# Keys made with tokens on partitions in a two-layer efficient-attention kernel

## The reference

```
xn = layernorm(x)
q, k, v = xn @ Wq + bq, xn @ Wk + bk, xn @ Wv + bv       # 512 x 512 each
k = k where the token is valid, else -inf (layer 0) or k - 1e6 (layer 1);  v = v * valid
q = softmax over the features of a head;   k = softmax over the tokens
att = k^T v for each head                                  # 16 heads of 32, then 8 of 64
y = q att;  h = layernorm(y) * (1 + scale(cond)) + shift(cond)
x = x + silu(h) @ Wout + bout
```

## Time and profile before

| what | value |
|---|---|
| median of 3 runs | 861.52 us (857.33 to 862.12) |
| the profiled execution | 857.14 us |
| its span in the trace | 855.1 us |
| PE busy | 838.2 us (98%) |
| DVE, ACT, POOL busy | 679.3, 603.1, 548.9 us |
| granted TensorE clock | full, in every slice |
| moved by DMA | 169.81 MB, 199 GB/s on average |

### The profile page before, as it was taken

The page is one execution under the profiler, slowest core; times in us unless marked ns, Lnnn a source line. Parts: engine busy times, 40 slices in busy tenths (PEclk is TensorE's granted clock), DMA queues, the critical chain, the costliest instruction groups (busy, mean ns, idle before and its releaser), DMA issues.

```text
span 855.1 us, 20095 instructions
## 1 busy us (share of the span) xinstructions
PE 838.2 (98%) x6659; PEld 719.9 (84%) x6659; DVE 679.3 (79%) x1362; ACT 603.1 (71%) x1442; POOL 548.9 (64%) x741
## 2 busy tenths in 40 slices
PE   7999999999999999999999999999999999999998
PEld 7778888888888888888878888888888888888886
DVE  6987778778788788778887887787788787787766
ACT  5376687686676776686876886776776686676665
POOL 3467766766766666766767667667667666765641
PEclk9999999999999999999999999999999999999999
DMA  8876676766667756555587556656566656566441
GB/s 309 286 225 201 201 218 199 228 216 205 195 210 208 233 197 199 179 165 175 169 247 233 185 172 200 201 180 201 179 204 201 202 186 189 178 194 211 142 160 62
DMA packets 139404, 169.81 MB, mean 199 GB/s; under 512 B 12302, under 2 KB 112006, under 8 KB 139302
## 3 DMA queue, kind: packets, MB, share of 16 engines
q1 hardware_dynamic: 138512, 167.56, 62.5%
q10 hardware_dynamic: 790, 0.98, 0.4%
HBM read 95.61 MB, written 72.88 MB: 197 GB/s over the span
## 4 chain that ended last, share of the span: by engine, by line
PE 83%; DMA 6%; DVE 4%; issue 2%; SPq 2%; POOL 1%; ACT 1%; DVEq 0%; POOLq 0%; ACTq 0%
PE PS L1152 72%; PE PS L1248 6%; PE PS L1232 3%; DMA X<-in_x 2%; DMA XT<-x_turned 1%; DMA x_turned<-XS 1%; DMA k_turned<-KT 1%; DMA QT<-qy_turned 1%; POOL XL L667 0%; SPq L400 0%; PE PS L1322 0%; DMA EK<-k_turned 0%; DVE BNX L1515 0%; PE PS L1276 0%; PE PS L1291 0%
## 5 line engine op out<-in xcount | busy, mean ns | idle before, releaser
L680 POOL TENSOR_TENSOR HL<-H,HH 128x512 fp32r<-128x512 f32 x60 | 77.5, 1292 | 185.3 <-ACT HH L916 185.3
L867 ACT ACTIVATE Z<-QT,FC,FA 128x128 f32<-128x128 f32 x240 | 99.0, 483 | 87.7 <-DMA QT<-qy_turned 87.7
L1152 PE MATMUL PS<-XH,WH_k 128*128 128x256 f32 x512 | 149.8, 293 | 0.7 <-DVE KN L1581 0.7
L1152 PE MATMUL PS<-XL,WH_k 128*128 128x256 f32 x512 | 144.8, 283 | 0.0
L1152 PE MATMUL PS<-XH,WL_k 128*128 128x256 f32 x512 | 144.8, 283 | 0.0
L953 ACT ACTIVATE XN<-X,NBX,RSX 128x512 f32<-128x512 f32 x60 | 48.8, 813 | 85.5 <-POOL NBX L629 85.5
L829 ACT ACTIVATE SK<-SK,KN 128x128 f32<-128x128 f32 x256 | 98.9, 387 | 10.7 <-DVE KN L1581 10.4
L1152 PE MATMUL PS<-WH_o,HH 128*128 128x512 f32 x248 | 101.3, 408 | 2.0 <-issue 1.9
L1152 PE MATMUL PS<-WH_v,XH 128*128 128x512 f32 x256 | 100.8, 394 | 0.0
L1152 PE MATMUL PS<-WH_q,XH 128*128 128x512 f32 x256 | 100.7, 393 | 0.0
L1152 PE MATMUL PS<-WL_v,XH 128*128 128x512 f32 x256 | 100.3, 392 | 0.0
(11 more groups left out here) (171 smaller groups left out, 2106.6 us busy)
## 6 DMA issues: line engine op xcount, KB each, us to landing
qy_turned<-QS SPq DMA_DIRECT2D x60, 512.0 KB, 2.9
QT<-qy_turned SPq DMA_DIRECT2D x240, 128.0 KB, 3.1
EK<-k_turned SPq DMA_DIRECT2D x128, 128.0 KB, 2.8
x_turned<-XS SPq DMA_DIRECT2D x30, 512.0 KB, 3.3
XT<-x_turned SPq DMA_DIRECT2D x120, 128.0 KB, 3.5
k_turned<-KT SPq DMA_DIRECT2D x52, 256.0 KB, 3.8
out_x<-X SPq DMA_DIRECT2D x31, 256.0 KB, 3.2
X<-in_x SPq DMA_DIRECT2D x11, 512.0 KB, 5.3
```

The costliest lines, as they stand in the source:

```text
L680: eng.tensor_tensor(hl_of(o), h_of(o), hh_of(o).bitcast(F32), ALU.subtract).then_inc(pool_hl, 1)
L867: z = eng.activation(z_of(o)[:, c * P:c * P + P].rearrange("p (q n) -> p q n", q=Q), src, ACT.Identity, bias=FC[l][:, c, b:b + 1], scale=F ...
L1152: mm = eng.matmul(dst, left[a](c), right[b](c), start=(c == 0 and a + b == 0), stop=(c == C - 1 and a == 1))
```

## The change

`keys(i)` now computes one tile's keys with tokens on partitions and features in the columns, through `project_x`, as values and queries do: 12 matmuls of 512 columns. ACT copies the bank to SK and adds the tile's mask, which is now one number for each token (`keep_keys`). The maxima over tokens go across partitions: DVE turns SK in 32 x 32 blocks (KT) and reduces each to 16 numbers (`key_maxima`, PM), PE transposes PM of a pair of tiles (`turn_max`), DVE reduces over the four groups of tokens and rounds as the key bias would (`row_maxima`, NM, 32 x 32), SP writes NM to memory and reads it back onto all 128 partitions (`write_max`, `spread_max`, MX, 128 x 1024). POOL subtracts MX (`shift_keys`), ACT takes one exponential of 512 columns (`exp_k`), and SK is used in attention where it lies.

Sums are no longer taken before attention. Each head's values have a column of ones beside them (VV is 33 or 65 columns a head), so attention's last column is the sum; DVE divides after attention (`scale_heads`, into HT), and POOL spreads HT over the head's place in ATT by multiplying it with a 0/1 pattern DG (`heads`), two instructions of 256 columns. The zeroing of PSUM, the masks in MB, EK and its transfers are gone. The lists are rewritten in even and odd steps; attention of all tiles from 4 to 61 is done in pairs.

```diff
             def keys(i):
 
-                g, p = divmod(i, 2)
-                l = i // B
+                g, t = divmod(i, 2)
...
-                    eng.wait_ge(dve_ka, i - 1 if i in (2, B + 2) else i)
-                xs = [lambda c: XH[g % 2][:, c, :], lambda c: XL[g % 2][:, c, :]]
-                for cc in range(2):
-                    f = (2 * p + cc) * P
-                    ws = [lambda c: WH[0][:, c, f:f + P], lambda c: WL[0][:, c, f:f + P]]
-                    dst = bank(bank_k(i), cc * PAIR, PAIR)
-                    mm = split_product(dst, ws, xs, fresh=(4 * l if i % B == 0 and cc == 0 else None))
-                mm.then_inc(pe_k, 1)
+                    eng.wait_ge(act_ka, i - 1 if i == 2 else i)
+                project_x(i, 0, bank(bank_k(i)), pe_k)
...
+            def turn_max(g):
+                eng.wait_ge(dve_pm, 2 * g + 2)
+                if g == 0:
+                    eng.wait_ge(act_xf, 3)
+                else:
+                    eng.wait_ge(dve_hd, max(2 * g - 1, 2))
+                eng.transpose(PS[0:D // 16, B_ATT, 0:P], PM[:, :, :].rearrange("p t n -> p (t n)"), ident[:, :])\
+                   .then_inc(pe_pm, 1)
...
+            def even_step(s):
+                keys(s)
+                values(s)
+                for j in attention_at(s):
+                    attention(j)
+                keys(s + 1)
+                queries(s)
+                output(s - 4)
+                turn_max(s // 2)
+                mix(s - 2)
+            def odd_step(s):
+                values(s)
...
+                queries(s)
...
+                output(s - 4)
+                mix(s - 2)
...
+            def key_maxima(i):
...
+                then(eng.transpose(KT[:, :].rearrange("p (a n) -> p a n", n=32),
+                                   SK[:, i % 3, :].rearrange("p (a n) -> p a n", n=32)))
+                eng.wait_ge(pe_pm, g)
+                eng.tensor_reduce(PM[:, t, :], KT[:, :].rearrange("p (a n) -> p a n", n=32), AX.X, ALU.max)\
+                   .then_inc(dve_pm, 1)
...
+            def row_maxima(g):
...
+                then(eng.tensor_reduce(NM[:, :], PS[0:D // 16, B_ATT, 0:P].rearrange("p (q n) -> p n q", q=Q), AX.X, ALU.max))
+                then(eng.tensor_tensor(NM[:, :], NM[:, :], bk, ALU.add))
+                eng.tensor_tensor(NM[:, :], NM[:, :], bk, ALU.subtract).then_inc(dve_km, 1)
...
+            def shift_keys(i):
+                eng.wait_ge(ld_mx, 16 * (i // 2 + 1))
+                sk = SK[:, i % 3, :]
+                eng.tensor_tensor(sk, sk, MX[:, i % 2, :], ALU.subtract).then_inc(pool_kn, 1)
...
+            def write_max(g):
+                eng.wait_ge(dve_km, g + 1)
+                eng.dma_start(KD, NM[:, :]).then_inc(st_km, 16)
+            def spread_max(g):
+                eng.wait_ge(st_km, 16 * (g + 1))
+                eng.wait_ge(pool_kn, 2 * g)
+                src = KD.rearrange("(o a) n -> o (a n)", o=1)
+                eng.dma_start(MX[:, :, :].rearrange("p t n -> p (t n)"), src.partition_broadcast(P)).then_inc(ld_mx, 16)
```

More of the change, by code:

```diff
@@ L742, in _ @@
-            for s in range(5, B - 1):
-                step(s)
-            add_bo(31)
-            root_y(28)
-            root_x(36)
-            split_low(eng, 4, [1])
-            x_low(33)
-            normalise_keys(31)
-            mask_of_keys(16)
-            queries(31)
-            h_low(27)
+            def odd_step(s):
+                h_low(s - 4)
+                root_y(s - 3)
+                if s > 5:
+                    heads(s - 2)
+                x_low(s + 2)
+                for n in stats_at(s):
+                    root_x(n)
+                shift_keys(s - 1)
+                shift_keys(s)
+                queries(s)
+                if s == 5:
+                    heads(s - 2)
@@ L753, in _ @@
+            odd_step(5)
+            for s in range(6, B - 2, 2):
+                even_step(s)
+                odd_step(s + 1)
+            even_step(30)
+            x_low(33)
+            split_low(eng, 4, [1])
+            h_low(27)
+            root_y(28)
+            heads(29)
+            queries(31)
+            shift_keys(30)
+            shift_keys(31)
+            root_y(29)
+            heads(30)
+            root_x(37)
             h_low(28)
-            root_y(29)
-            normalise_keys(32)
@@ L788, in _ @@
+            add_bo(33)
+            even_step(34)
+            odd_step(35)
             split_low(eng, 7, [1])
-            root_x(41)
             split_low(eng, 7, [3])
-            normalise_keys(36)
-            queries(36)
-            x_low(38)
-            for s in range(B + 5, NT - 2):
-                step(s)
+            for s in range(B + 4, NT - 2, 2):
+                even_step(s)
+                odd_step(s + 1)
             add_bo(62)
             root_y(59)
+            heads(60)
@@ L1024, in step, with odd_step @@
                     norm_x(n)
+                exp_k(s - 2)
+                exp_k(s - 1)
+                keep_keys(s)
+                norm_y(s - 3)
                 film(s - 4)
+                exp_q(s - 2)
+                values(s)
+                h_high(s - 4)
+                keep_keys(s + 1)
+                x_turned(s + 2)
+                film(s - 3)
+            def odd_step(s):
+                if s == 5:
+                    film(1)
+                h_high(s - 4)
+                exp_q(s - 2)
+                for n in norm_at(s):
+                    norm_x(n)
+                x_turned(s + 2)
@@ L1026, in step @@
                 norm_y(s - 3)
-                x_turned(s + 2)
-                h_high(s - 4)
                 if s in FILM_SLOTS:
                     conditioning_sums(FILM_SLOTS.index(s))
-                exp_k(s)
-                exp_q(s - 2)
-                heads(s - 2)
                 values(s)
-            for s in range(5, B - 1):
-                step(s)
-            norm_x(35)
+            odd_step(5)
+            for s in range(6, B - 2, 2):
+                even_step(s)
+                odd_step(s + 1)
@@ L1123, in _ @@
             values(t2)
+            exp_k(62)
             exp_q(t1)
-            heads(t1)
+            exp_k(63)
             norm_y(t0)
@@ L1391, in _ @@
             count()
+            turn_max(0)
             keys(2)
@@ L1408, in _, with even_step, odd_step @@
             keep_busy(B_K, 2)
-            def step(s):
-                keys(s)
+            keys(4)
+            queries(4)
+            values(4)
+            output(0)
+            attention(2)
+            keys(5)
+            mix(2)
+            values(5)
+            turn_max(2)
+            queries(5)
+            attention(3)
+            output(1)
+            mix(3)
+            def even_step(s):
+                keys(s)
+                values(s)
[6 more added lines that the diff above has]
+                mix(s - 2)
+            def odd_step(s):
                 values(s)
@@ L1417, in step @@
                     conditioning_fold(FILM_SLOTS.index(s))
-                for j in attention_at(s):
-                    attention(j)
                 output(s - 4)
                 mix(s - 2)
-            keys(4)
-            queries(4)
-            values(4)
-            output(0)
-            attention(2)
-            mix(2)
-            for s in range(5, B - 1):
-                step(s)
-            keys(31)
+            for s in range(6, B - 2, 2):
+                even_step(s)
+                odd_step(s + 1)
+            even_step(30)
             values(31)
@@ L1971, in _ @@
+            even_step(34)
+            odd_step(35)
+            split_low(eng, 7, [0])
+            split_low(eng, 7, [2])
+            for s in range(B + 4, NT - 2, 2):
+                even_step(s)
+                odd_step(s + 1)
             add_x(57)
```

791 lines of the change are left out of this document (344 added, 447 removed).

## The result

The changed kernel takes 910.25 us (median of 4 runs, 908.46 to 911.63), the kernel before 859.42 us (4 runs, 856.64 to 862.12): a ratio of 1.059, 95% interval 1.0543 to 1.0638. The forecast was 859.0 us, its range ended at 873. In the profiled executions the span grew from 855.1 to 907.5 us, by 52.4.

A forecast was written before the change was run, and what follows sets the result against it. PE's own list was taken as the bound, busy 98% of the span. Terms -8.0 + 7.0 - 1.0 - 2.5 + 1.5 + 0.5 = -2.5 us gave 854.6 against the profiled 857.14, 859.0 us on the median's footing; range 848 to 873.

The forecast's parts named there:

- Keys, -8.0: PE's keys: 12 matmuls in 2.72 us instead of 24 in 2.85, 0.13 us for each of 64 tiles, -8.0 us.
- Lone transposition, +7.0: PE's turn_max between output and mix, 32 in all, taken at 0.22 us each: +7.0 us (2.9 to 9.0).
- The term for attention, -1.0: Fewer tiles with lone attention, six instead of eleven, save changes of matmul kind on PE: -1.0 us (0 to -1.5).
- What lies beside PE in a pair, nothing: DVE, ACT, POOL, SP and the maxima's chain in steady pairs cost nothing while PE is the cover.
- The start, +1.5 (0 to +5): First maxima, written behind the output weight, delay attention(0) from 50.66 to 53 to 56 us: +1.5 us.
- The turn, -2.5 (-3.8 to +2): Between the layers, waits on EK, ATT and KN, 3.8 us, lose their cause; new waits possible: -2.5 us.
- The end, +0.5 (0 to +2): Between turn_max(31) and attention(62), the maxima's chain of 10.4 us against 10.1 us of PE work: +0.5 us.
- Slower at the ends: Rival: first and turn's maxima late behind weights, start +5, turn +2, end +2; 868.5 us on the median; chance 0.08.
- POOL's loop: Rival: POOL's in-order list delays steady pairs, 0.5 us in each of 29, 14.5 us; 873.5 on the median; chance 0.20.
- The test I named for the late start: Sign of a late start: attention(0) later than 53 us.
- The chances: Forecast within 0.5% 0.38, faster 0.34, POOL's loop 0.20, late ends 0.08; so faster 0.34, same 0.38, slower 0.28.

The follow-up runs named there:

- Run 8: Changed kernel with one edit: in even steps POOL has h_low(s-4) ahead of heads(s-2) and the second add_bo behind heads; 918.87 us, ratio 1.069.
- Runs 4: Changed kernel with fillers (PE transposing the identity) put into three long waits of the start; 903.76 us, ratio 1.053.
- 6: Changed kernel with many places in the start's DVE, ACT and POOL lists moved together, nothing removed; 899.06 us, ratio 1.048.
- run 11: Order of run 10 with a load of query weights and four more places moved, in step 5 and at the turn; 890.2 us, ratio 1.037.
- runs 3: Changed kernel with the turn's lists reordered: DVE's values(32), values(33) and both stat_x, and POOL's h_low(28), moved ahead; 910.83 us, ratio 1.061.
- run 12: Order of run 11 without the chain of maxima (transposition, row maxima, write, spread), the subtraction taking zeros; 887.89 us, ratio 1.036.
- run 13: Order of run 11 with low parts of the second layer's key, value and query weights over 4 columns instead of 512; 886.91 us, ratio 1.035.
- run 14: Order of run 11 with turn_max(16) and mix(30) between queries(32) and queries(33) on PE, DVE's queries(32) moved ahead; 887.79 us, ratio 1.034.
- run 15: Order of run 14 with turn_y(29), write_qy(32), film(29), h_mul(29) and h_low(29), between mix(29) and output(29), moved forward; 890.91 us, ratio 1.037.
- run 1: Changed kernel without turn_max, row_maxima, write_max and spread_max, POOL subtracting zeros; 903.11 us, ratio 1.052.
- run 10: Changed kernel with places at start, turn and end moved, even steps untouched, nothing removed or added; 890.39 us, ratio 1.037.

## Why the prediction was wrong

**Keys, -8.0: right.** 12 matmuls in 2.72 us, pairs 0.13 us a tile shorter in PE's list, at the full clock.

**Lone transposition, +7.0: the value chosen was too high.** Its next start is 0.10 to 0.11 us later, so 32 cost 3.2 to 3.5 us. The upper bound of 0.28 came from a single transposition of 56 columns in the first 11 us of the kernel, and why it took so long there is not shown; the lower bound, 0.09, was near the price. The pair without a wait, -0.21 us, fits keys (-0.26) and transposition (+0.10) to 0.05 us. The term for attention, -1.0, is too small to be seen among these.

**What lies beside PE in a pair, nothing: right, but thin.** DVE and POOL were as forecast (the cover of five products and two mixes is 15.2 us by its own terms, not 15.4, which changes nothing) and the steady stages came out at +0.8 and -0.2 us. Yet waits of a microsecond before output took back what PE's list had gained, 0.2 us in each of some 25 pairs, 5 us. I had no term for that. Run 8 shows how near the edge POOL's order is.

**The start, +1.5 (0 to +5): wrong, +26.0.** Here the prediction failed. The step "the first maxima are late, so attention(0) is" looked at one chain. The maxima came earlier than I had them and attention(0) was on time. What I did not do is take each list of the start in order and ask what is queued behind the operation that waits for the maxima. Three such places (`keep_keys(3)` and `key_maxima(3)` ahead of `values(2)`; the subtractions ahead of `h_low(0)`; `heads(3)` last in POOL's step 5) cost 16.5 us of PE's waits, and the clock about 6 more. Runs 4 and 6 show both: places gave back 14 us by values(6), and 10 us by values(8) in run 11.

**The turn, -2.5 (-3.8 to +2): wrong in sign, +21.1.** I counted only the waits that lose their cause and one new risk on SP, not what stands behind each wait in the rewritten lists. The change had rewritten the lists of the turn: blocks of a kind stand two in a row on PE, and DVE has `values(32)` and `stat_x(37)` behind splits of weights. Reordered, the turn cost 6 to 7 us less (runs 3 and 11), but only 2 to 3 of these are PE's idle time; the rest is the granted clock, for which the prediction had no term here either. What holds the other 14 to 15 us, 12.9 of them idle time in run 11, is not settled. It isn't the maxima (run 12), nor the weights' low parts (run 13), nor one query block behind the other (run 14), nor one row of hand-overs (run 15). That several rows are late by the same 3 to 4 us at once is argued from the moving wait, not shown. In the profile of run 11 the chain that ended last goes at the turn through y's way over memory twice (write and read, 3.70 and 4.72 us, then 3.26 and 2.75); no run shortened that. A turn with the order of the kernel before was not tried, since the even and odd steps around it don't fit that order.

**The end, +0.5 (0 to +2): mis-sized, +4.9.** I priced only the maxima there, and they cost nothing (run 1: the same idle time without them). What had no cover was the way from attention to mix. Before, ACT copies the bank: 0.60 us. Now DVE divides, and in the last two tiles places the result in ATT itself, 0.17 + 0.86 us, and does so behind other work. Tile 63 before and in the changed kernel:

```profile
838.31 0.60 ACT L902 ACTIVATE ATT<-PS 128x512 f32<-128x512 f32 x1
...
839.01 1.14 PE L1248 MATMUL PS<-ATT,EQ 128*128 128x132 f32 x8 [0.76 <-ACT EQ L847]
```

```profile
889.20 0.17 DVE L1579 RECIPROCAL RE<-PS 128x4 f32<-128x4 f32 x1
889.41 0.86 DVE L1584 TENSOR_TENSOR ATT<-PS,RE 64x256 f32<-64x256 f32 x2
...
890.37 2.10 PE L1221 MATMUL PS<-ATT,EQ 128*128 128x132 f32 x8 [2.52 <-issue]
```

With both moved ahead in DVE's list (run 10) the stage costs 2.4 us. Half of the difference is PE's idle time, 3.13 instead of 4.34 us; the other half is the clock, 1.00 instead of 0.93, and five runs with the end as it was have it at 1.00 too, at a cost of 3.6 to 3.7 (run 14 has the moved order at 0.91 and costs 4.0). The rest, 2.2 us of idle time more than before, fits the longer way.

**The rivals.** "Slower at the ends" had the right places at a sixth of the price, +9 us in sum against 52, and a chance of 0.08. "POOL's loop" had 0.20 and did not happen in this order. The test I named for the late start, attention(0) later than 53 us, would have cleared the start while it lost 26 us: it looked at the chain, not at what stands behind it.

**The chances** leaned on the steady loop, which makes up three quarters of the time (649 of 855 us between the marks above) and almost none of the loss.

No version here beats the kernel before; the best orders take 888 to 891 us against 857 to 859. So order gives back 20 of the 52 us; of the other 32, about half of them at the turn, no run here gives back more than 1 to 4 us. Even without any stall the change could have given only about 5 us.

## What to carry to other kernels

When an edit puts a long wait into an in-order queue, list what stands behind the waiting instruction in the written-out parts (start, turns, end) as well as in the loop: here the loss was there (52.0 us, against 0.6 in the loop). Read the granted clock of each stage beside its delay, or a change of the clock is taken for a gain of places. Budget the delay by the same block in both traces, stage by stage, before you form a theory; and expect that a wait removed by a move shows up at the next block, so move a whole row and measure by the budget, not by the wait.

## What the runs showed of the hardware

- **The clock behind a wait.** After waits of 5.35, 5.55 and 5.62 us PE came back at starts 0.43 us apart, the level of 1.2 GHz, and went back to 0.23 within a block or so; at the turn and the end the mean clock is 0.93 as well. Filling the waits of the start kept it at 1.00 there and gave 6 us. I had no term for it. The Trainium skill, "TensorE: Matmul & The Clock Gate", section "Part 1: The HAM clock gate", says that the throttled state is the default and activity releases it; the rows agree.
- **A lone transposition.** Its record lasts 0.27 us, and yet the next matmul starts 0.10 to 0.11 us after it. The same page, section "Part 4: PE-mode transpose", gives about 275 ns in a kernel's context, for bf16; that is the record's length here, in fp32, and not the place it takes on PE.
- **A small write can be slow.** The maxima of a pair are 4 KB; their 32 writes take 1.3 us from issue to landing in the median, but the first one, issued 0.43 us behind the 1 MB load of the output weight, took 6.33 us. In the kernel before, x_turned's write took 7.94 us at that place. That the load is the cause was not tested. SP's queue:

```profile
36.85 0.39 SPq L391 DMA_DIRECT2D STAGE<-in_wo  x1
37.28 0.50 SPq L454 DMA_DIRECT2D k_maxima<-NM  x1
43.63 0.34 SPq L461 DMA_DIRECT2D MX<-k_maxima  x1
```
